# Reordering the last two batches of a Flamingo layer: one engine queue's steps against another's

## The reference

```python
def _act_quant(x):
    scale = 127.0 / jnp.clip(jnp.max(jnp.abs(x), axis=-1, keepdims=True), 1e-05)
    xq = jnp.clip(jnp.round(x * scale), -128.0, 127.0) / scale
    return x + jax.lax.stop_gradient(xq - x)
def _bitlinear(x, w):
    return jnp.einsum('bsi,oi->bso', _act_quant(x), _weight_quant(w))
gate = jax.nn.silu(_bitlinear(x, w_gate))
up = _bitlinear(x, w_up)
return _bitlinear(gate * up, w_down)
...
x = x + jnp.tanh(g_xattn[0]) * _L0_xattn_ref(_layernorm(x, axis=-1), ctx_1024, ...)
x = x + jnp.tanh(g_ffn[0]) * _L0_ffn_ref(_layernorm(x, axis=-1), L0_ffn_w_gate, L0_ffn_w_up, L0_ffn_w_down)
```

## Time and profile before

| | us |
|---|---|
| median of three runs | 508.52 |
| lowest, highest | 507.63, 509.7 |
| the profiled execution | 509.66 |
| its span, first to last instruction | 507.9 |
| mean granted TensorE clock | 0.982 |
| TensorE, VectorE, ScalarE, GpSimd busy | 483.6, 437.5, 374.5, 248.6 |

### The profile page before, as it was taken

How to read it: one execution, slowest core, us unless ns; L and a number is a source line. 1 busy time by engine, 2 the same in 40 slices (tenths; PEclk the granted TensorE clock), 3 DMA queues, 4 the chain that set the end, 5 groups by cost and what they waited for, 6 DMA issues and landing times.

```text
span 507.9 us, 9896 instructions
## 1 busy us (share of the span) xinstructions
PE 483.6 (95%) x3088; PEld 400.6 (79%) x3088; DVE 437.5 (86%) x1002; ACT 374.5 (74%) x611; POOL 248.6 (49%) x389
## 2 busy tenths in 40 slices
PE   8898999999999999999999999999999999999593
PEld 8686888988877987788877887788868887897352
DVE  6989988787989899898989799897899888957874
ACT  3583869867778778687878588686768687886874
POOL 7391364189125484248525484247415912656511
PEclk9997999999999999999999999999999999999789
DMA  5863251321112330222312430242113111330001
GB/s 185 184 216 122 43 203 47 62 62 57 53 21 43 97 94 21 43 63 72 95 23 62 84 92 13 43 63 73 53 25 80 65 22 21 63 84 3 21 22 42
DMA packets 64018, 34.72 MB, mean 68 GB/s; under 512 B 41696, under 2 KB 63456, under 8 KB 63968
## 3 DMA queue, kind: packets, MB, share of 16 engines
q1 hardware_dynamic: 63136, 34.09, 26.4%
q10 hardware_dynamic: 832, 0.00, 0.1%
HBM read 20.46 MB, written 4.19 MB: 49 GB/s over the span
## 4 chain that ended last, share of the span: by engine, by line
PE 76%; ACT 8%; DVE 6%; DMA 5%; issue 3%; POOL 1%; SPq 0%; DVEq 0%; ACTq 0%; POOLq 0%
PE ps L2516 47%; PE ps L2676 8%; PE ps L2576 7%; PE ps L2698 4%; DMA w_bit<-place_c 3%; PE ps L2585 3%; PE ps L2533 2%; DMA work<-in_L_xattn_wo_dram 2%; PE ps L2524 2%; DVE cols L1749 1%; PE ps L2593 1%; ACT place_c L1010 1%; DVE work L1743 1%; PE ps L2611 1%; ACT work L993 1%
## 5 line engine op out<-in xcount | busy, mean ns | idle before, releaser
L559 POOL TENSOR_TENSOR mv<-mv,cols 128x2 f32<-128x2 f32 x64 | 13.2, 206 | 162.6 <-DVE mv L1615 162.4
L2516 PE MATMUL ps<-w_hi,h_hi 128*128 128x256 f32 x256 | 75.9, 297 | 0.2
L2516 PE MATMUL ps<-w_lo,h_hi 128*128 128x256 f32 x256 | 71.5, 279 | 0.0
L2516 PE MATMUL ps<-w_hi,h_lo 128*128 128x256 f32 x256 | 71.4, 279 | 0.0
L942 ACT ACTIVATE h_hi<-ps,cols 128x512 fp32r<-128x512 f32 (+1 forms) x72 | 45.5, 637 | 13.6 <-PE ps L2516 8.6
L2516 PE MATMUL ps<-n1T_hi,w_hi 128*128 128x512 f32 (+1 forms) x144 | 54.1, 376 | 0.1
L1669 DVE RECIPROCAL ps<-ps 128x512 f32<-128x512 f32 x16 | 53.7, 3358 | 0.1
L2516 PE MATMUL ps<-n1T_lo,w_hi 128*128 128x512 f32 (+1 forms) x144 | 53.3, 370 | 0.0
L2516 PE MATMUL ps<-n1T_hi,w_lo 128*128 128x512 f32 (+1 forms) x144 | 53.2, 370 | 0.0
L2516 PEld LDWEIGHTS ps<-w_hi,h_hi 128*128 128x128 f32 x256 | 48.2, 188 | 3.3 <-DVE h_lo L1704 1.0
L988 ACT ACTIVATE work<-ps,cols 128x1024 f32<-128x1024 f32 x32 | 35.7, 1116 | 19.1 <-PE ps L2676 10.1
(11 more groups left out here) (186 smaller groups left out, 1493.0 us busy)
## 6 DMA issues: line engine op xcount, KB each, us to landing
x_in<-in_x_dram SPq DMA_DIRECT2D x16, 256.0 KB, 3.0
emb<-in_ctx_dram SPq DMA_DIRECT2D x16, 256.0 KB, 2.9
work<-in_x_dram SPq DMA_DIRECT2D x8, 512.0 KB, 3.7
out_dram<-work SPq DMA_DIRECT2D x16, 256.0 KB, 2.2
work<-in_L_xattn_w_dram SPq DMA_DIRECT2D x2, 1024.0 KB, 9.7
work<-in_L_ffn_w_gate_dram SPq DMA_DIRECT2D x1, 1024.0 KB, 5.5
work<-in_L_ffn_w_up_dram SPq DMA_DIRECT2D x1, 1024.0 KB, 5.6
place_c<-in_L_ffn_w_down_dram SPq DMA_DIRECT2D x1, 1024.0 KB, 7.6
```

Of the source, the lines that this page charges most:

```text
L2516: last = nc.tensor.matmul(dst, lhsT, rhs, start=(i == 0 and not begun), stop=(i == n - 1 and ends))
```

## The change

The order of steps at the end of three queues, and the banks that go with it. SyncE's and GpSimd's queues stay as they are. On TensorE `xq_rows(7, 0)`, `gate(7, 0)` and `gate(7, 1)`, `up(7, 0)` and `up(7, 1)` and `xq_rows(7, 1)` stand earlier against the down products and transposes of batch 6. On ScalarE `product_scales(7, 0)` and `token_quantise(7, 0)` go ahead of `hq_columns(6, 1)`, `xq_columns(7, 0)` ahead of `hq_columns(6, 2)`, while `quantise(6, 3)` and `hq_columns(6, 3)` go back. On VectorE the scales and the second statistics of batch 7 go ahead of the products of batch 6, and the last tile's reduction ahead of two outputs. No step is added or left out.

```diff
-    ... ("xqP", 0): (0, 0, 0, 0, 0, 0, 7, 4),
-    ... ("gate", 0): (6, 6, 2, 6, 2, 6, 6, 4), ("up", 0): (2, 6, 2, 6, 0, 6, 6, 2),
-    ("hqP", 0): (0, 0, 0, 0, 0, 0, 1, 4), ("down", 0): (5, 4, 5, 4, 6, 1, 1, 4),
-    ... ("up", 1): (6, 0, 0, 0, 2, 2, 4, 4), ("hqP", 1): (0, 0, 0, 0, 0, 0, 0, 5),
-    ("down", 1): (1, 1, 1, 1, 6, 5, 0, 5), ("gate", 2): (2, 6, 2, 6, 0, 6, 6, 6), ("up", 2): (2, 6, 2, 6, 2, 2, 0, 0),
-    ("hqP", 2): (0, 0, 0, 0, 0, 0, 1, 6), ("down", 2): (1, 1, 1, 1, 4, 1, 1, 6),
-    ("gate", 3): (2, 6, 2, 6, 2, 2, 2, 6), ("up", 3): (6, 2, 6, 2, 0, 6, 4, 2), ("hqP", 3): (0, 0, 0, 0, 0, 0, 1, 6),
-    ("down", 3): (2, 6, 2, 6, 5, 7, 1, 6)}
+    ... ("xqP", 0): (0, 0, 0, 0, 0, 0, 7, 7),
+    ... ("gate", 0): (6, 6, 2, 6, 2, 6, 6, 2), ("up", 0): (2, 6, 2, 6, 0, 6, 6, 4),
+    ("hqP", 0): (0, 0, 0, 0, 0, 0, 1, 0), ("down", 0): (5, 4, 5, 4, 6, 1, 1, 0),
+    ... ("up", 1): (6, 0, 0, 0, 2, 2, 4, 2), ("hqP", 1): (0, 0, 0, 0, 0, 0, 1, 1),
+    ("down", 1): (1, 1, 1, 1, 6, 5, 1, 1), ("gate", 2): (2, 6, 2, 6, 0, 6, 6, 4), ("up", 2): (2, 6, 2, 6, 2, 2, 0, 6),
+    ("hqP", 2): (0, 0, 0, 0, 0, 0, 0, 6), ("down", 2): (1, 1, 1, 1, 4, 1, 0, 6),
+    ("gate", 3): (2, 6, 2, 6, 2, 2, 2, 2), ("up", 3): (6, 2, 6, 2, 0, 6, 4, 4), ("hqP", 3): (0, 0, 0, 0, 0, 0, 1, 7),
+    ("down", 3): (2, 6, 2, 6, 5, 7, 1, 7)}
@@ ScalarE
             silu(6, 3)
-            hq_columns(6, 1)
             product_scales(7, 0)
             token_quantise(7, 0)
+            hq_columns(6, 1)
+            xq_columns(7, 0)
             hq_columns(6, 2)
-            quantise(6, 3)
-            xq_columns(7, 0)
             normalise(7, 3, 1)
             silu(7, 0)
-            hq_columns(6, 3)
+            quantise(6, 3)
             token_quantise(7, 1)
             silu(7, 1)
             product_scales(7, 1)
+            hq_columns(6, 3)
             xq_columns(7, 1)
             silu(7, 2)
             hq_columns(7, 0)
@@ VectorE
             product_scale(6, 1)
             product(6, 2)
             token_max(7, 0)
+            token_scales(7, 0)
             product_scale(6, 2)
-            token_scales(7, 0)
+            tile_stats(7, 3, 2)
+            tile_stats(7, 3, 3)
+            mean_variance(7, 3, 1)
             product(6, 3)
-            tile_stats(7, 3, 2)
             product_scale(6, 3)
             output(6, 1)
-            tile_stats(7, 3, 3)
-            mean_variance(7, 3, 1)
-            output(6, 2)
             token_max(7, 1)
             token_scales(7, 1)
+            output(6, 2)
             product(7, 0)
             product_scale(7, 0)
             output(6, 3)
...
             product(7, 3)
+            product_scale(7, 3)
             output(7, 0)
             output(7, 1)
-            product_scale(7, 3)
             output(7, 2)
             output(7, 3)
@@ TensorE
             hq_rows(6, 1)
+            xq_rows(7, 0)
             down(6, 1)
+            gate(7, 0)
             hq_rows(6, 2)
-            xq_rows(7, 0)
+            gate(7, 1)
+            up(7, 0)
             down(6, 2)
-            gate(7, 0)
+            up(7, 1)
             hq_rows(6, 3)
-            up(7, 0)
-            gate(7, 1)
-            up(7, 1)
+            xq_rows(7, 1)
             down(6, 3)
-            xq_rows(7, 1)
             gate(7, 2)
             up(7, 2)
             hq_rows(7, 0)
-            up(7, 3)
             gate(7, 3)
             down(7, 0)
+            up(7, 3)
             hq_rows(7, 1)
```

More of the change, by code:

```diff
@@ L60 @@
     ("g", 5): (0, 0, 0, 0, 0, 0, 0, 1), ("g", 6): (0, 0, 0, 0, 0, 0, 0, 5), ("g", 7): (0, 0, 0, 0, 0, 0, 0, 3),
[1 row of a table removed]
-    ("xqP", 1): (0, 0, 0, 0, 0, 0, 2, 0), ("gate", 0): (6, 6, 2, 6, 2, 6, 6, 4), ("up", 0): (2, 6, 2, 6, 0, 6, 6, 2),
-    ("hqP", 0): (0, 0, 0, 0, 0, 0, 1, 4), ("down", 0): (5, 4, 5, 4, 6, 1, 1, 4),
-    ("gate", 1): (6, 0, 0, 0, 2, 2, 6, 6), ("up", 1): (6, 0, 0, 0, 2, 2, 4, 4), ("hqP", 1): (0, 0, 0, 0, 0, 0, 0, 5),
-    ("down", 1): (1, 1, 1, 1, 6, 5, 0, 5), ("gate", 2): (2, 6, 2, 6, 0, 6, 6, 6), ("up", 2): (2, 6, 2, 6, 2, 2, 0, 0),
-    ("hqP", 2): (0, 0, 0, 0, 0, 0, 1, 6), ("down", 2): (1, 1, 1, 1, 4, 1, 1, 6),
-    ("gate", 3): (2, 6, 2, 6, 2, 2, 2, 6), ("up", 3): (6, 2, 6, 2, 0, 6, 4, 2), ("hqP", 3): (0, 0, 0, 0, 0, 0, 1, 6),
-    ("down", 3): (2, 6, 2, 6, 5, 7, 1, 6)}
[1 row of a table added]
+    ("xqP", 1): (0, 0, 0, 0, 0, 0, 2, 0), ("gate", 0): (6, 6, 2, 6, 2, 6, 6, 2), ("up", 0): (2, 6, 2, 6, 0, 6, 6, 4),
+    ("hqP", 0): (0, 0, 0, 0, 0, 0, 1, 0), ("down", 0): (5, 4, 5, 4, 6, 1, 1, 0),
+    ("gate", 1): (6, 0, 0, 0, 2, 2, 6, 6), ("up", 1): (6, 0, 0, 0, 2, 2, 4, 2), ("hqP", 1): (0, 0, 0, 0, 0, 0, 1, 1),
+    ("down", 1): (1, 1, 1, 1, 6, 5, 1, 1), ("gate", 2): (2, 6, 2, 6, 0, 6, 6, 4), ("up", 2): (2, 6, 2, 6, 2, 2, 0, 6),
+    ("hqP", 2): (0, 0, 0, 0, 0, 0, 0, 6), ("down", 2): (1, 1, 1, 1, 4, 1, 0, 6),
+    ("gate", 3): (2, 6, 2, 6, 2, 2, 2, 2), ("up", 3): (6, 2, 6, 2, 0, 6, 4, 4), ("hqP", 3): (0, 0, 0, 0, 0, 0, 1, 7),
+    ("down", 3): (2, 6, 2, 6, 5, 7, 1, 7)}
 PAIRED = ("gate", "up")
```

## The result

The changed kernel took 510.19 us in the median of seven runs (509.7 to 512.51), the kernel before 509.37 us in the same comparison (507.63 to 510.16). The ratio is 1.0034, with a 95% interval of 1.0019 to 1.0048: some 1.7 us slower (1.0 to 2.4). I go by the ratios. Forecast were +1.0 us and 509.5 us. So the sign is right, the slowdown is clear of the noise, and the forecast lies at the lower edge of what was measured.

The account below looks back on a forecast made before the run. The tail's VectorE chain up to quantise(7, 3) was taken as the bound. Product(7, 1) 1.62 us late, less 0.68 for the last reduction, with 0.05: about +1.0 on the 508.52 median, 509.5 us; range 507.3 to 510.9.

Parts of the forecast that it names:

- The kernel's tail: Only the part behind 471 us is open; quantise(7, 3)'s start sets the end, 7.4 us later.
- (a): VectorE, last tile: product_scale(7, 3) ahead of two outputs saves 0.68 us on the path.
- the banks cost nothing: New PSUM bank table: bank waits end on work long done or are hidden by data waits, so no cost.
- (b): VectorE: batch 7's scales and second statistics ahead of batch 6's products; product(6, 3) near 478.0, no cost and no gain.
- (c) and (d): ScalarE and TensorE queues: hq_columns(6, 2) at 482.68 instead of 479.64, product(7, 0) gains 0.37 us, product(7, 1) 1.62 late.
- The last move: Tail's end: the move of GpSimd's tile 2 may hold the last quantise for 0.05 us.
- The 5.0 us of unbroken work: TensorE from 478.26: full clock returns after this much work, at 483.3, leaving the transposes hq_rows(6, 2) slow.
- the second fall: Rival: clock falls again in TensorE's sparse 486.8 to 490.4, down(6, 3) 0.83 longer: +1.8, 510.3 us; chance 0.13.
- early return: Rival: clock is back by hq_rows(6, 2) or during gate(7, 0): 508.6 to 509.1 us; chance 0.17.
- full clock: Rival: TensorE's clock never falls, hq_columns(6, 2) 2.04 earlier: about -1.1, 507.4 us; chance 0.08.
- second fall to the end: Rival: clock falls again and stays at half from 490.39, product(7, 3) at 501.4: +5.4, 513.9 us; chance 0.04.
- a queue without cost: Rival: ScalarE's queue behind hq_columns(6, 2) costs nothing, only the 0.68 and 0.37 us gains count: 507.5 us; chance 0.06.

Follow-up runs that it names:

- kernels 3: Kernel before with only product_scale(7, 3) moved ahead of output(7, 0) and output(7, 1): 508.52 us, ratio 0.9993.
- Kernel 7: Kernel before with product_scale(7, 3) ahead of the two outputs, and hqP and down of batch 7's tile 3 in bank 7 instead of 6: 507.57 us, ratio 0.9971.
- kernel 5: Changed kernel with 18 and 10 unread transposes around hq_rows(6, 1) and 14 between xq_rows(7, 1) and down(6, 3): 508.82 us, ratio 0.9990.
- kernel 10: Changed kernel with hq_rows(6, 2) directly behind down(6, 1) and 14 unread transposes between xq_rows(7, 1) and down(6, 3): 508.98 us, ratio 1.0006.
- kernel 9: Changed kernel with output(6, 3) behind product_scale(7, 1) and 14 unread transposes between xq_rows(7, 1) and down(6, 3): 509.69 us, ratio 1.0017.
- 11: Changed kernel with output(6, 3) behind product_scale(7, 1) and three TensorE stretches filled with 18, 10 and 14 unread transposes: 507.81 us, ratio 0.9975.
- kernel 2: Changed kernel with hq_rows(6, 2) directly behind down(6, 1), ahead of gate(7, 0): 510.55 us, ratio 1.0034.
- kernel 1: Changed kernel with output(6, 3) behind product_scale(7, 1) instead of ahead of product(7, 1): 511.76 us, ratio 1.0054.
- kernel 6: Changed kernel with only 14 unread transposes between xq_rows(7, 1) and down(6, 3): 510.42 us, ratio 1.0026.
- the second profile of the changed one: Changed kernel, unaltered, profiled and timed again in another comparison with the kernel before: 510.49 us, ratio 1.0036.
- kernel 8: Kernel before with product_scale(7, 3) first, tile 3 in bank 7, and 18 and 8 unread transposes around hq_rows(6, 1): 507.64 us, ratio 0.9966.

## Why the prediction came out as it did

**The kernel's tail.** Right: nothing before `product(6, 2)` is involved, and the end follows `quantise(7, 3)` by 7.4 us.

**(a), the last reduction.** Right in size, 0.68 us (498.52 - 497.28 = 1.24 instead of 1.92). But "the banks cost nothing" was half of the truth. In the new table they cost nothing; kernels 3 and 7 show that without the new bank of tile 3, 0.45 us of this gain would have gone into a wait for `output(7, 2)`. I had followed the waits of the new table alone.

**(b), scales and statistics early.** Right: no cost, no gain. `product(6, 3)` starts 1.1 us later, and no one waits for it.

**(c) and (d), the queues.** Right to 0.03 us up to `product(7, 1)`. The gate product is early, and `silu(7, 0)` isn't. What each part of the chain is worth in the profiles: 2.08 us the half clock (kernel 5), 0.74 us the place of `hq_rows(6, 2)` (kernel 10), 0.55 that of `output(6, 3)` (9 and 11). These overlap and don't add up.

**The last move.** The 0.05 us allowed for GpSimd's tile 2 and its move was 0.18: the last reduction is 0.97 us late by the common clock (498.52 + 1.01 against 498.56), the last quantise 1.15. `hq_columns(7, 2)` starts at 499.63 and the quantise 1.01 later. GpSimd was through at 498.60; the prediction had not seen that TensorE was at `down(7, 1)` until 498.98.

**The clock, the step that failed.** The fall stayed, as said. The 5.0 us of unbroken work taken for the return is no constant: full speed was back 4.4 us after the begin of such work (481.6, from 477.22 on) in one profile of the changed kernel, 5.1 in the other, and 2.4 in kernels 2 and 9. But the second fall was given 0.13, "not much more than before the fall at 475.7", and `down(6, 3)` was put into the sum with 1.04 us. Of the two profiles of the changed kernel one has it, with 1.87 us for this product and 0.98 us in all; so has that of kernel 1, whose TensorE runs alike up to there. The mechanism and its place were on the list; its weight was too low, and the sum took the case without it as if it were the mean: +1.0 forecast, +1.15 without a second fall, +2.13 with one, +1.7 and +1.8 timed. That second falls make up the rest is what kernel 6 and the mean clocks point to; it is not proven. The other rivals (early return, full clock, second fall to the end, a queue without cost) did not occur in the two profiles; an early return is in that of kernel 9, where `gate(7, 0)` took 1.37 us and ScalarE waited 3.08.

**The base and the resolution.** The 509.5 us stood on the median of three runs, 508.52. In the comparison the kernel before had 509.37, and 509.5 would have been no slowdown to speak of; so it is the +1.0 that can be held against the measurement. The 0.5% given as the least difference that timed runs can tell was too coarse: the intervals here reach 0.5 to 0.7 us to either side.

By the Trainium skill, "TensorE: Matmul & The Clock Gate", section "What's actually happening", the moment of a change of clock shifts from run to run. The runs agree, with a wider shift than the 0.5 us to either side that it gives: counted from `product(6, 2)`, the first fall came 1.0 us behind it in kernel 2, 2.9 in the kernel before and 3.8 in the second profile of the changed one. So one profile of a stage with a gap in TensorE's work is one draw of several.

What is open: whether half is the share of second falls (only two profiles of this kernel, and intervals that overlap), how much the order costs with the clock up, and why kernels 1 and 7 were 0.6 and 0.8 us further out than their profiles, and kernel 2 by 2.2. All these profiles are also compared with a single one of the kernel before. Kernel 7, an edit of one line and one bank on the kernel before, is faster than both kernels.

## What to carry to other kernels

Moving a step of the next batch ahead pays only if its consumer's queue is free when it arrives; here it delayed a short step on which one engine's whole queue hung. In a list written by hand, look for the step that stands in front of the bottleneck's next piece and waits for a far-off chain. Where TensorE has a gap near the place of a change, work out the sum for each clock that can come about and weigh them; don't take the one profile's. And before an aid such as the filling decides between two orders, give it to both.

## What the runs showed of the hardware

- The granted clock fell again behind a stretch in which TensorE idled 2.06 us at a time at most and had done two sets of transposes; it didn't fall in another execution of the same program with the same gap. With 14 unread transposes (1.70 to 1.75 us) in this gap it stayed up in all five profiles that had them.
- With 3.2 us of unread transposes on both sides of `hq_rows(6, 1)` the clock stayed up there and fell in a later gap of 1.39 us, which followed one down product (1.03 us) and an earlier gap of 1.07 us (kernel 8).
